# Adding the causal mask of the diagonal score tiles on VectorE, in PSUM, instead of by matmuls

## The chip, the cores and the metric

One core of one Trainium2 chip runs the whole program in one launch. The metric is the device time of an execution in microseconds (us). Three executions of the kernel before took 1168.46, 1168.53 and 1172.29 us; the median is 1168.53 us.

## The reference, cut to what matters

A block of four sequences of 1024 tokens (width 256): layer norm with modulation, attention, a residual, a second layer norm, a mixture of eight experts, a second residual. The change lies in the attention. There are 16 heads of 16 features. Of each head's query, key and value one feature per token is kept, the largest in magnitude; each query then keeps its 64 best allowed keys:

```python
q = _sparsify_last_dim_topk(proj(wq), feature_keep)     # feature_keep = 1
k = _sparsify_last_dim_topk(proj(wk), feature_keep)
v = _sparsify_last_dim_topk(proj(wv), feature_keep)
scores = einsum('bhqd,bhkd->bhqk', q, k) / sqrt(16)
causal = triu(ones((T, T), dtype=bool), k=1)
scores = where(causal[None, None], -inf, scores)         # a key later than the query is left out
topk_vals, topk_idx = lax.top_k(scores, 64)
attn = softmax(scatter of topk_vals, -inf elsewhere)
out = einsum('bhqk,bhkd->bhqd', attn, v)
```

## The kernel before, in words

**Tiles and groups.** The attention of one sequence b (0 to 3) and four heads g (0 to 3) is one of 16 groups, gi = 4 b + g. Keys lie on the 128 partitions, queries along the free dimension. A group has nine score units (table `UNITS`, line 330); a unit is 512 query columns, made of one or two pieces (i, t0, w): key tile i, queries from t0, width w. A piece whose first query is its tile's first key (t0 = 128 i) starts with a diagonal tile, 128 x 128, in which the keys later than the query must not count. There are eight such pieces in a group: two in units 0, 2 and 8, one in units 1 and 3. Units 4 to 7 have none.

**TensorE.** `scores(gi, u)` (line 436) writes the unit's four heads into two double banks of PSUM: half a = 0 holds heads 0 and 1, half a = 1 heads 2 and 3. For a piece it issues the products of query and key for four heads (line 451), then a product with `over` that pushes unselected keys down (455), and for a diagonal piece four matmuls of 128 columns (460) that add the tile `late`: 0 where the query may see the key, -1e30 where it may not. The last matmul of a half raises `f_full`. `late` is bf16 in SBUF and is filled once, before the attention starts.

**The ring.** Six banks are three double banks used in turn (`ring_at`, `begin`, line 369). A score unit takes two of them, other pieces of work (`chosen`, `project`, transposes) one each. The next unit therefore can't begin before ScalarE has read half a = 0 of the last one. Bank 6 gathers the output, bank 7 serves small work one piece at a time in a chain (`f_mfull`, `f_mfree`).

**ScalarE** waits for `f_full` and takes the exponential of half a unit at once (128 x 1024, line 850) into `p_buf`; its completion raises `f_free`. TensorE then multiplies `p_buf` with the values (`pv`, line 482).

**VectorE** works its own queue in program order (the loop from line 1166 on). For group gi this is: `mask` on unit 1 (two instructions of line 1068, after unit 1's exponentials and a matmul group `chosen`), `one_feature` for the next sequence (992, 997), `norm_stats`, or `second_norm` (1121, 1125) of the sequence before, `out_rows_of` (1073 to 1076), `key_counts` of the next group (1015, 1017), another `one_feature`, `mask` on unit 4, `keys` (1024 to 1032), `queries` (1037 to 1039), `zero_rank` (1044, 1047), `losers` (1054) and `negatives` (1060). Which of them exist depends on g: `one_feature` in g = 1 and 2 of b = 0 to 2 (four times a group); `second_norm` in g = 3 of b > 0; `norm_stats` in g = 0 (b < 3) and g = 1; `residual` (1101 to 1112) in g = 0 of b > 0, its second half just before `negatives`. TensorE waits for `mask` on unit 4 before `scores(gi, 5)`, since it frees the double banks, and for `losers` before the matmuls `lost` (432, 433) that end a group.

Every order is written out by hand; no planner or scheduler moves anything. These lines say the order around the change on VectorE, for a group's first third:

```python
                    mask(gi, 0, 0)
                    mask(gi, 0, 1)
                    if tiles:
                        one_feature(b + 1, t0)
                    if g == 0 and pre:
                        norm_stats(b + 1, 0)
                    if g == 3 and post:
                        second_norm(b - 1, 0)
                    if gi:
                        out_rows_of(gi - 1, 1)
                    if more:
                        key_counts(n)
```

Of the kernel before, what the change touches and what calls it, by code (L numbers as in the profile page):

```python
# [5 lines left out]
ALU = mybir.AluOpType  # L6
# [7 lines left out]
P = 128  # L14
# [6 lines left out]
HG = 4  # L21
# [11 lines left out]
def build_kernel(nc, x, wq, wk, wv, wo, router_w, router_b, w1, b1, w2, b2, c, wmod, out):  # L33
    with ExitStack() as ctx:
# [3 lines left out]
        def sem(name):  # L38
            return ctx.enter_context(nc.semaphore(name))
# [280 lines left out]
        TINY = 1e-30  # L320
        FAR = 2.0 ** 60

        f_const, f_ones = sem("f_const"), sem("f_ones")
        f_x, f_xr, f_xfree = (sem(n) for n in ("f_x", "f_xr", "f_xfree"))
        f_var, f_rstd, f_xhat, f_hT, f_yev, f_one, f_keep, f_cnt = (sem(n) for n in (
            "f_var", "f_rstd", "f_xhat", "f_hT", "f_yev", "f_one", "f_keep", "f_cnt"))
# [13 lines left out]
        NU = len(UNITS)  # L340
# [2 lines left out]


        ring_at, m_at, pv_at = {}, {}, {}

        def buf(u):
            q = ring_at[u] % 3
# [2 lines left out]
        def full_of(u):  # L351
            return f_full[ring_at[u] % 3], ring_at[u] // 3 + 1
# [10 lines left out]
        with nc.Block() as blk:  # L363
            @blk.tensor
            def _(pe):
# [70 lines left out]
                def scores(gi, u):  # L436
                    par = gi % 2
                    if u == 0:
                        pe.wait_ge(f_kp, gi + 1)
                        pe.wait_ge(f_uq, gi + 1)  # L440
                    for a in range(2):
                        begin(("S", gi, u, a))
                    lo = 0
                    for i, t0, w in UNITS[u]:
                        diag = t0 == P * i
                        last = (i, t0, w) == UNITS[u][-1]
                        for h in range(HG):
                            r = slice(32 * h, 32 * h + 32)
                            o = buf(("S", gi, u, h // 2))[:, h % 2, lo:lo + w]
                            key = ks[r, par, :] if i == 0 else kd[r, par, P * i:P * i + P]  # L450
                            pe.matmul(o, key, qx[r, par, t0:t0 + w], start=True, stop=False)  # L451
                        for h in range(HG):
                            r = slice(32 * h, 32 * h + 32)
                            o = buf(("S", gi, u, h // 2))[:, h % 2, lo:lo + w]
                            m = pe.matmul(o, over[r, :], qm[r, par, t0:t0 + w], start=False, stop=not diag)  # L455
                            if h % 2 and last and not diag:
                                m.then_inc(full_of(("S", gi, u, h // 2))[0], 1)
                        for h in range(HG * diag):
                            o = buf(("S", gi, u, h // 2))[:, h % 2, lo:lo + P]
                            m = pe.matmul(o, identb[:, :], late[:, :], start=False, stop=True)  # L460
                            if h % 2 and last:
                                m.then_inc(full_of(("S", gi, u, h // 2))[0], 1)
                        lo += w
# [342 lines left out]
            def _(act):  # L806
# [36 lines left out]
                def exps(gi, u):  # L843
                    j = NU * gi + u - PB
                    if j >= 0:
                        act.wait_ge(f_pv, pv_at[j // NU, j % NU])
                    for a in range(2):
                        w = ("S", gi, u, a)
                        act.wait_ge(*full_of(w))
                        act.activation(p_of(gi, u)[:, 2 * a:2 * a + 2, :], buf(w), ACT.Exp, scale=0.25).then_inc(free_of(w)[0], 1)  # L850

                def out_bank(gi, c):
# [86 lines left out]
            def _(dve):  # L939
# [118 lines left out]
                def negatives(n):  # L1058
                    m_full(("W", n))
                    dve.tensor_tensor(neg_in[:, :, :], ps[:, 7, :].rearrange("p (h t) -> p h t", h=HG),  # L1060
                                      thr_w[:, :].unsqueeze(1).to_broadcast([P, HG, P]), ALU.is_ge).then_inc(f_mfree, 1)

                def mask(gi, c, a):
                    u = ("Z", gi, c, a)
                    dve.wait_ge(*free_of(("S", gi, FIRST[c], a)))
                    dve.wait_ge(*full_of(u))
                    pb = p_of(gi, FIRST[c])[:, 2 * a:2 * a + 2, :]
                    dve.scalar_tensor_tensor(pb, buf(u), 1.0, pb, ALU.is_gt, ALU.mult).then_inc(free_of(u)[0], 1)  # L1068
# [95 lines left out]
                for gi in range(GA):  # L1164
                    b, g = divmod(gi, NG)
                    n = gi + 1
                    more, pre, post = n < GA, b + 1 < B, b > 0
                    tiles = pre and g in (1, 2)
                    t0 = 4 * (g - 1)

                    if g == 0 and post:
                        gate_weights(b - 1)
                        take_weights(b - 1)
                    mask(gi, 0, 0)
                    mask(gi, 0, 1)
                    if tiles:
                        one_feature(b + 1, t0)
                    if g == 0 and pre:
# [8 lines that stand above are left out]
                        normalize(b + 1, 0)  # L1187
                    if tiles:
                        one_feature(b + 1, t0 + 1)
                    mask(gi, 1, 0)  # L1190
                    mask(gi, 1, 1)
                    if g == 3 and post:
                        second_norm(b - 1, 1)
                    if g == 1 and pre:
                        norm_stats(b + 1, 1)
                    if more:
                        keys(n)
                    if tiles:
                        one_feature(b + 1, t0 + 2)
                    out_rows_of(gi, 0)  # L1200
                    if g == 0 and post:
                        take_mod(b - 1)
                    if more:
                        queries(n)
                    if g == 0 and post:
                        residual(b - 1, 0)
                    if more:
                        zero_rank(n)
                    if g == 1 and pre:
                        normalize(b + 1, 1)  # L1210
                    if g == 0 and pre:
                        modulate(b + 1, 0)
                    if tiles:
                        one_feature(b + 1, t0 + 3)
                    if g == 3 and pre:
                        feature_limits(b + 1)
                    if more:
                        losers(n)
                    if g == 0 and post:
                        residual(b - 1, 1)  # L1220
                    if g == 1 and pre:
                        modulate(b + 1, 1)
                    if g == 3 and post:
                        router_max(b - 1)
                    if more:
                        negatives(n)
                    if g == 3 and post:
                        router_share(b - 1)
# [762 lines left out]
```

## Time and profile before

| | |
|---|---|
| median of three executions | 1168.53 us |
| profiled execution, its time | 1168.28 us |
| its span, first to last instruction | 1166.5 us |
| mean granted TensorE clock | 0.905 of full |
| busy: TensorE, VectorE, ScalarE, GpSimd | 84%, 56%, 43%, 16% |
| attention groups | from about 116 to 787 us of the span |

A busy share is an average over stages. The first 116 us prepare weights and the first sequence, the last 380 us are the experts; the change touches only what lies between. A row of a view of groups gives line, engine, operation, tiles, shapes, count, busy us and mean ns of one, then the idle time before and what ended it. A row of the timeline gives the start, the duration over all instructions merged in it, engine, line, tiles, and in brackets the idle time before it and what ended that.

### The profile page before, as it was taken

Reading aid. Unit: us, or ns where it says so; the run is one execution under the profiler, and the core shown is the slowest. Engines: PE = TensorE matmul, PEld = TensorE weight load, DVE = VectorE, ACT = ScalarE, POOL = GpSimd, SP = SyncE. Lnnn points to the kernel's source line nnn. Section 1 sums busy time; section 2 is a strip of 40 time slices with the busy share of each in tenths; the row PEclk is TensorE's granted clock in tenths of the full one; section 3 lists DMA queues with packets and bytes.
Section 4 is the critical chain, followed back from the end, with each engine's and each line's share of the span. In section 5 each row is a group of like instructions: output and inputs, shape, how many; then the busy total and the mean of one; then the engine's idle time right before and its main releaser. Section 6 shows DMA issues by size and latency. Waiting matters only on the chain. (4 is left out here: it accounts for less than half of the span.)

```text
span 1166.5 us, 19195 instructions
## 1 busy us (share of the span) xinstructions
PE 978.1 (84%) x7592; PEld 545.0 (47%) x7592; DVE 652.7 (56%) x1378; ACT 506.7 (43%) x680; POOL 186.3 (16%) x280
## 2 busy tenths in 40 slices
PE   6453899999999999899998999998501799999996
PEld 4222344444444445454445453446401476666664
DVE  2445657756657764759666556643367555554441
ACT  0043666777466774556675646660000111111120
POOL 1231003200012200013110000000000434334322
PEclk9675999999899998999999899997555799999998
DMA  2200000000010001010000210002271244342211
GB/s 91 73 18 1 1 19 20 1 2 1 1 55 19 1 1 41 34 55 2 1 2 1 74 37 1 2 1 75 72 278 68 57 105 109 106 109 40 24 15 22
DMA packets 35456, 47.75 MB, mean 41 GB/s; under 512 B 2010, under 2 KB 31778, under 8 KB 35234
## 3 DMA queue, kind: packets, MB, share of 16 engines
q1 hardware_dynamic: 29218, 37.93, 9.7%
q0 software_dynamic: 6144, 8.52, 4.4%
q8 instruction: 64, 1.05, 0.4%
q14 instruction: 30, 0.25, 0.1%
HBM read 33.73 MB, written 12.72 MB: 40 GB/s over the span
## 5 line engine op out<-in xcount | busy, mean ns | idle before, releaser
L850 ACT ACTIVATE p_buf<-ps 128x1024 f32<-128x1024 f32 x288 | 279.2, 1023 | 188.3 <-PE ps L460 124.0
L451 PE MATMUL ps<-qx,kd 32*128 32x512 f32 (+3 forms) x1280 | 146.3, 527 | 23.6 <-DVE p_buf L1068 19.8
L482 PE MATMUL ps<-p_buf,vv 128*17 128x512 f32 (+3 forms) x1664 | 157.0, 479 | 0.0
L1824 ACT ACTIVATE h_t<-ps,b_t 128x512 f32<-128x512 f32 x64 | 44.0, 687 | 244.3 <-PE ps L1764 244.3
L1068 DVE SCALAR_TENSOR_TENSOR p_buf<-ps,p_buf 128x1024 f32<-128x1024 f32 x64 | 76.1, 1221 | 81.6 <-ACT p_buf L850 75.5
L1764 PE MATMUL ps<-tok_t,w_sb 128*128 128x512 f32 x256 | 114.1, 604 | 0.0
L1774 PE MATMUL ps<-w_sb,h_t 128*128 128x256 f32 x512 | 112.5, 380 | 0.8 <-ACT h_t L1824 0.8
L1774 PEld LDWEIGHTS ps<-w_sb,h_t 128*128 128x128 f32 x512 | 96.6, 190 | 15.3 <-ACT h_t L1824 1.6
L397 PE MATMUL ps<-w_t,h_t 128*128 128x512 f32 (+1 forms) x256 | 93.7, 514 | 8.8 <-DVEq L986 8.6
L451 PEld LDWEIGHTS ps<-qx,kd 32*128 32x128 f32 x1280 | 52.5, 189 | 64.5 <-issue 47.4
L1764 PEld LDWEIGHTS ps<-tok_t,w_sb 128*128 128x128 f32 x256 | 49.2, 194 | 59.2 <-issue 58.9
L784 POOL TENSOR_TENSOR qk<-y_val,y_one 128x512 f32<-128x512 f32 x32 | 37.1, 1159 | 238.2 <-DVE y_one L997 238.2
L397 PEld LDWEIGHTS ps<-w_t,h_t 128*128 128x128 f32 x256 | 48.4, 197 | 56.4 <-issue 51.4
L455 PE MATMUL ps<-qm,over 32*128 32x512 bf16 (+3 forms) x768 | 68.2, 328 | 0.0
L817 ACT ACTIVATE y_abs<-ps 128x768 f32<-128x768 f32 x32 | 25.9, 810 | 93.8 <-PE ps L397 87.4
L1728 POOL DMA_INDIRECT out_dram<-ctr,ids x32 | 50.7, 1583 | 98.1 <-issue 98.1
L482 PEld LDWEIGHTS ps<-p_buf,vv 128*17 128x17 f32 x1664 | 34.5, 97 | 55.6 <-issue 48.3
L460 PEld LDWEIGHTS ps<-late,identb 128*128 128x128 bf16 x512 | 29.9, 100 | 53.2 <-issue 53.2
L776 POOL TENSOR_TENSOR rstd<-var_e,half_neg 128x8 f32<-128x8 f32 x4 | 6.5, 1636 | 296.9 <-DVE var_e L1112 296.9
L1876 DVE TENSOR_TENSOR eo<-ps,b_sb 128x256 f32<-128x256 f32 x32 | 13.6, 425 | 72.0 <-PE ps L1774 71.4
L992 DVE TENSOR_REDUCE y_mx<-y_abs 128x48 f32<-128x768 f32 x32 | 30.5, 952 | 41.5 <-ACT y_abs L817 41.5
L460 PE MATMUL ps<-late,identb 128*128 128x128 bf16 x512 | 52.5, 227 | 0.0
(249 smaller groups left out, 1444.9 us busy)
## 6 DMA issues: line engine op xcount, KB each, us to landing
w_sb<-in_L_ffn_w_dram SPq DMA_DIRECT2D x16, 1024.0 KB, 8.6
h_table<-xr SPq DMA_DIRECT2D x4, 1056.0 KB, 4.6
x_in<-in_L_attn_x_dram SPq DMA_DIRECT2D x8, 512.0 KB, 3.5
xr<-in_L_attn_x_dram SPq DMA_DIRECT2D x4, 1024.0 KB, 5.5
out_dram<-xr SPq DMA_DIRECT2D x4, 1024.0 KB, 4.8
wmod_sb<-in_L_wmod_dram SPq DMA_DIRECT2D x1, 1536.0 KB
b_sb<-in_L_ffn_b_dram SPq DMA_DIRECT2D x1, 1024.0 KB, 9.5
gb_sb<-gb_table SPq DMA_DIRECT2D x1, 512.0 KB, 10.2
```

Source lines behind the costliest of these rows:

```text
L397: m = pe.matmul(buf(u)[:, bank, 0:n], h_t[:, k, (t % 4) * P:(t % 4 + 1) * P], w_t[:, k, lo:lo + n], start=k == 0, stop=k == KD - 1)
L451: pe.matmul(o, key, qx[r, par, t0:t0 + w], start=True, stop=False)
L455: m = pe.matmul(o, over[r, :], qm[r, par, t0:t0 + w], start=False, stop=not diag)
L460: m = pe.matmul(o, identb[:, :], late[:, :], start=False, stop=True)
L482: m = pe.matmul(ps[32 * h:32 * h + HD + 1, 6, o:o + w], vv[:, (gi // NG) % 2, i, HG * (gi % NG) + h, :], p_of(gi, u)[:, h, lo:lo + w], sta ...
L784: pool.tensor_tensor(qk[:, t], y_val[:, 0:2 * NH], y_one[:, 0:2 * NH], ALU.mult)
L850: act.activation(p_of(gi, u)[:, 2 * a:2 * a + 2, :], buf(w), ACT.Exp, scale=0.25).then_inc(free_of(w)[0], 1)
L1068: dve.scalar_tensor_tensor(pb, buf(u), 1.0, pb, ALU.is_gt, ALU.mult).then_inc(free_of(u)[0], 1)
L1728: pool.indirect_dma_start(out_rows, bass.IndirectOffsetOnAxis(ids[:, e, k:k + 1], 0), ctr[:, e % 2, k, :], None, compute_op=ALU.add).then_ ...
L1764: m = pe.matmul(ps[:, L1_BANKS[f % 3], :], w1_sb[:, e % WB, k, f * P:(f + 1) * P], tok_t[:, e % 2, k, :], start=k == 0, stop=k == KD - 1)
L1774: m = pe.matmul(ps[:, 4 + q % 2, 0:D], h1_t[:, f, q * P:(q + 1) * P], w2_sb[:, e % WB, f, :], start=f == 0, stop=f == FO - 1)
L1824: act.activation(h1_t[:, f, :], ps[:, L1_BANKS[f % 3], :], ACT.Relu, bias=b1_t[:, e * FO + f:e * FO + f + 1]).then_inc(s_h1, 1)
```

## The change

The matmuls with `late` (line 460) go. `scores` now raises `f_full` with its `over` product. VectorE adds `late` to the two heads of a half in place in PSUM, one instruction of 128 x 2 x 128 for each diagonal piece and half, and raises a new semaphore `f_late`; for units 0, 1, 2, 3 and 8 ScalarE waits for that instead of `f_full`. So 512 matmuls of TensorE leave and 256 instructions of VectorE come, 32 and 16 a group. Their places in VectorE's queue are those of the five calls of `set_late`. What is computed stays the same.

```diff
+        DIAG = tuple(u for u in range(NU) if any(t0 == P * i for i, t0, w in UNITS[u]))
+        late_at = {(gi, u, a): 2 * (len(DIAG) * gi + DIAG.index(u)) + a + 1 for gi in range(GA) for u in DIAG for a in range(2)}
...
-                            m = pe.matmul(o, over[r, :], qm[r, par, t0:t0 + w], start=False, stop=not diag)
-                            if h % 2 and last and not diag:
-                                m.then_inc(full_of(("S", gi, u, h // 2))[0], 1)
-                        for h in range(HG * diag):
-                            o = buf(("S", gi, u, h // 2))[:, h % 2, lo:lo + P]
-                            m = pe.matmul(o, identb[:, :], late[:, :], start=False, stop=True)
+                            m = pe.matmul(o, over[r, :], qm[r, par, t0:t0 + w], start=False, stop=True)
                             if h % 2 and last:
                                 m.then_inc(full_of(("S", gi, u, h // 2))[0], 1)
...
-                        act.wait_ge(*full_of(w))
+                        if u in DIAG:
+                            act.wait_ge(f_late, late_at[gi, u, a])
+                        else:
+                            act.wait_ge(*full_of(w))
...
+                def set_late(gi, u):
+                    for a in range(2):
+                        w = ("S", gi, u, a)
+                        dve.wait_ge(*full_of(w))
+                        lo = 0
+                        for i, t0, n in UNITS[u]:
+                            if t0 == P * i:
+                                s = buf(w)[:, :, lo:lo + P]
+                                m = dve.tensor_tensor(s, s, late[:, :].unsqueeze(1).to_broadcast([P, 2, P]), ALU.add)
+                            lo += n
+                        m.then_inc(f_late, 1)
...
+                    set_late(gi, 0)
+
                     if g == 0 and post:
                         gate_weights(b - 1)
                         take_weights(b - 1)
+                    set_late(gi, 1)
                     mask(gi, 0, 0)
                     mask(gi, 0, 1)
+                    set_late(gi, 2)
+                    set_late(gi, 3)
                     if tiles:
                         one_feature(b + 1, t0)
...
                     if tiles:
                         one_feature(b + 1, t0 + 3)
+                    set_late(gi, 8)
...
                     if more:
                         losers(n)
```

How this moves VectorE's queue is seen best in its rows. First the early part of a group with g = 2, before: `mask` on unit 1, `one_feature`, `out_rows_of`, `key_counts`, `one_feature`, `mask` on unit 4.

```order
L1068 SCALAR_TENSOR_TENSOR p_buf<-ps,p_buf 128x1024 x2
L992 TENSOR_REDUCE y_mx<-y_abs 128x48
L997 TENSOR_TENSOR y_one<-y_abs,y_mx 128x768
L1073 TENSOR_TENSOR z_lo<-z_lo,ps 128x16
L1074 RECIPROCAL o_inv<-ps 128x16
L1076 TENSOR_TENSOR o_tok<-ps,o_inv 128x4x64
L1015 TENSOR_SCALAR k_not<-kd 128x1024
L1017 SCALAR_TENSOR_TENSOR left<-k_not,minus 128x1024
L992 TENSOR_REDUCE y_mx<-y_abs 128x48
L997 TENSOR_TENSOR y_one<-y_abs,y_mx 128x768
L1068 SCALAR_TENSOR_TENSOR p_buf<-ps,p_buf 128x1024 x2
```

The same stretch now (lines below the new function are 12 higher, so `mask` is line 1080):

```order
L1071 TENSOR_TENSOR ps<-ps,late 128x2x128 x6
L1080 SCALAR_TENSOR_TENSOR p_buf<-ps,p_buf 128x1024 x2
L1071 TENSOR_TENSOR ps<-ps,late 128x2x128 x6
L992 TENSOR_REDUCE y_mx<-y_abs 128x48
L997 TENSOR_TENSOR y_one<-y_abs,y_mx 128x768
L1085 TENSOR_TENSOR z_lo<-z_lo,ps 128x16
```

Six additions stand ahead of the first `mask` (units 0 and 1) and six behind it (four for unit 2, two for unit 3), so everything from `one_feature` on comes after unit 3's scores. Next the end of a group with g = 0 and b > 0 on VectorE and the start of the group behind it, before: `zero_rank`, `modulate`, `losers`, second half of `residual`, `negatives`, `mask`.

```order
L1047 RECIPROCAL wk_r<-z_rank 128x128
L983 TENSOR_SCALAR h_t<-ps,mod_t 128x512 x2
L1054 SCALAR_TENSOR_TENSOR lw<-ps,y_mx,tie 128x128 x4
L1101 TENSOR_TENSOR xr<-ps,xr 128x4x256
L1106 BN_STATS st<-xr 128x6 x4
L1109 BN_AGGR mv<-st 128x2 x4
L1112 TENSOR_SCALAR var_e<-mv 128x8
L1060 TENSOR_TENSOR neg_in<-ps,thr_w 128x512
L1068 SCALAR_TENSOR_TENSOR p_buf<-ps,p_buf 128x1024 x2
```

And now:

```order
L1047 RECIPROCAL wk_r<-z_rank 128x128
L983 TENSOR_SCALAR h_t<-ps,mod_t 128x512 x2
L1071 TENSOR_TENSOR ps<-ps,late 128x2x128 x4
L1054 SCALAR_TENSOR_TENSOR lw<-ps,y_mx,tie 128x128 x4
L1113 TENSOR_TENSOR xr<-ps,xr 128x4x256
L1118 BN_STATS st<-xr 128x6 x4
L1121 BN_AGGR mv<-st 128x2 x4
L1124 TENSOR_SCALAR var_e<-mv 128x8
L1060 TENSOR_TENSOR neg_in<-ps,thr_w 128x512
L1071 TENSOR_TENSOR ps<-ps,late 128x2x128 x6
```

Unit 8's four additions stand ahead of `losers` in every group, and the next group's unit 0 is served only behind `residual` and `negatives`.

## Rows read from the trace of the kernel before

**Rows 1.** The page, part 1: busy us of each engine.
```profile
PE 978.1 (84%) x7592; PEld 545.0 (47%) x7592; DVE 652.7 (56%) x1378; ACT 506.7 (43%) x680; POOL 186.3 (16%) x280
```
**Rows 2.** Groups g = 2, 3, 0: length, busy PE, PEld, DVE, ACT, POOL, granted clock, DMA.
```profile
368.00:411.60 43.60, 41.89 (x371) 19.25 (x367) 29.25 (x38) 30.15 (x41) 8.39 (x9) 1.00 0.04 13
411.60:458.10 46.50, 41.78 (x401) 23.51 (x399) 27.41 (x52) 27.27 (x37) 0.00 (x0) 0.95 0.00 1
458.10:507.80 49.70, 46.65 (x399) 23.93 (x397) 30.26 (x62) 25.17 (x31) 1.01 (x1) 0.91 0.14 44
```
**Rows 3.** Groups of instructions by line.
```profile
L460 PE MATMUL ps<-late,identb 128*128 128x128 bf16 x512 | 52.5, 227 | 0.0
L1076 DVE TENSOR_TENSOR o_tok<-ps,o_inv 128x256 f32<-128x256 f32 x32 | 13.6, 425 | 2.4
```
**Rows 4.** Timeline of TensorE, unit 2 of the group g = 2, b = 1.
```profile
379.49 0.40 PE L460 MATMUL ps<-late,identb 128*128 128x128 bf16 x4
379.81 0.71 PE L451 MATMUL ps<-qx,kd 32*128 32x256 f32 x8
```
**Rows 5.** Timeline, units 0 and 1 of the last group.
```profile
754.79 0.93 PE L451 MATMUL ps<-qx,kd 32*128 32x384 f32 x8
...
757.02 1.94 ACT L850 ACTIVATE p_buf<-ps 128x1024 f32<-128x1024 f32 x2 [3.02 <-PE ps L460]
758.18 1.14 PE L451 MATMUL ps<-qx,ks 32*128 32x512 f32 x8 [0.17 <-ACT p_buf L850]
```
**Rows 6.** Timeline, group g = 2, b = 1, unit 3 to unit 5.
```profile
379.68 0.95 DVE L992 TENSOR_REDUCE y_mx<-y_abs 128x48 f32<-128x768 f32 x1 [2.17 <-ACT y_abs L817]
382.33 1.14 PE L451 MATMUL ps<-qx,kd 32*128 32x512 f32 x8
384.50 0.17 DVE L1073 TENSOR_TENSOR z_lo<-z_lo,ps 128x16 f32<-128x16 f32 x1 [2.76 <-PE ps L524]
391.07 2.35 DVE L1068 SCALAR_TENSOR_TENSOR p_buf<-ps,p_buf 128x1024 f32<-128x1024 f32 x2
392.44 1.14 PE L451 MATMUL ps<-qx,kd 32*128 32x512 f32 x8 [0.72 <-DVE p_buf L1068]
```
**Rows 7.** Timeline, end of the same group.
```profile
406.68 0.93 PE L451 MATMUL ps<-qx,kd 32*128 32x384 f32 x8
407.63 0.95 DVE L992 TENSOR_REDUCE y_mx<-y_abs 128x48 f32<-128x768 f32 x1 [0.60 <-ACT y_abs L817]
409.91 1.13 DVE L1054 SCALAR_TENSOR_TENSOR lw<-ps,y_mx,tie 128x128 bf16<-128x128 f32 x4 [0.22 <-PE ps L424]
411.09 0.23 PE L432 MATMUL ps<-upto,lw 128*128 128x128 bf16 x1 [0.24 <-DVE lw L1054]
```
**Rows 8.** Timeline, group g = 3, b = 1.
```profile
421.09 1.67 DVE L1121 SCALAR_TENSOR_TENSOR xr<-xr,mv,bc 128x256 f32<-128x256 f32 x4
425.96 0.17 DVE L1073 TENSOR_TENSOR z_lo<-z_lo,ps 128x16 f32<-128x16 f32 x1 [1.45 <-PE ps L524]
431.32 1.14 PE L451 MATMUL ps<-qx,kd 32*128 32x512 f32 x8 [0.99 <-DVE p_buf L1068]
447.00 1.13 DVE L1054 SCALAR_TENSOR_TENSOR lw<-ps,y_mx,tie 128x128 bf16<-128x128 f32 x4 [0.52 <-PE ps L424]
```
**Rows 9.** Timeline, group g = 0, b = 2, and the start of the next.
```profile
474.58 0.17 DVE L1073 TENSOR_TENSOR z_lo<-z_lo,ps 128x16 f32<-128x16 f32 x1 [2.34 <-PE ps L524]
482.54 1.14 PE L451 MATMUL ps<-qx,kd 32*128 32x512 f32 x8 [2.54 <-DVE p_buf L1068]
...
510.04 1.94 ACT L850 ACTIVATE p_buf<-ps 128x1024 f32<-128x1024 f32 x2 [6.26 <-PE ps L460]
510.86 0.68 DVE L1060 TENSOR_TENSOR neg_in<-ps,thr_w 128x512 bf16<-128x512 f32 x1
```
**Rows 10.** Stretches of 5 us around TensorE's wait of rows 9.
```profile
478.00:483.00 5.00, 2.46 (x18) 1.70 (x22) 4.88 (x8) 2.94 (x4) 0.00 (x0) 1.00 0.00 0
483.00:488.00 5.00, 5.00 (x37) 1.91 (x30) 4.27 (x6) 2.51 (x3) 0.00 (x0) 0.66 0.00 0
```

More of the change, by code:

```diff
@@ L321, in build_kernel @@
         FAR = 2.0 ** 60
-        f_const, f_ones = sem("f_const"), sem("f_ones")
+        f_const, f_ones, f_late = sem("f_const"), sem("f_ones"), sem("f_late")
         f_x, f_xr, f_xfree = (sem(n) for n in ("f_x", "f_xr", "f_xfree"))
@@ L444, in scores @@
                     for i, t0, w in UNITS[u]:
-                        diag = t0 == P * i
                         last = (i, t0, w) == UNITS[u][-1]
```

## The prediction

> **What bounds the kernel now.** I read the page first: TensorE is busy 84% of the span, VectorE 56% [rows 1]. The stretches then say what the average hides: in a group of the attention TensorE is busy 41.9 of 43.6 us, VectorE 29.3 [rows 2]. The reader is to see TensorE nearly full, and VectorE with a third of its time free. That makes the trade look sound: take work from the full engine, give it to the one with room. So the timeline has to say where TensorE does wait, since a shorter TensorE only moves such waits. It shows three. After unit 0 it waits 0.17 us for the exponential that frees a double bank [rows 5]. Before unit 5 it waits for VectorE's `mask`: 0.72 us in a group with g = 2, 0.99 in one with g = 3, 2.54 in one with g = 0 [rows 6, 8, 9]. Before `lost` it waits 0.24 us for `losers` [rows 7]. The last two are ends of long runs of VectorE in program order. VectorE's free time lies elsewhere, just ahead of instructions that wait for somebody: 2.17 us before `one_feature`, 2.76 before `out_rows_of` [rows 6]. The question is thus not whether 7 us of additions a group fit, but what they push behind them.
>
> **What is removed.** Four `late` matmuls begin 0.32 us before the next work begins [rows 4]; the 227 ns of one [rows 3] is its latency, and they overlap. 128 such sets are 128 x 0.32 = 41 us of TensorE, 2.6 a group. That is the most that could be won, and only where TensorE, not a wait, sets the pace.
>
> **What is added.** The trace has no addition in place in PSUM. The nearest row reads the same 256 elements from PSUM beside an SBUF operand: 425 ns [rows 3]. Its destination is SBUF, not PSUM. The bound below is 0.28 us, what `losers` takes per instruction in a run (four of half the size in 1.13 us [rows 7]); above, 0.6, should a write to PSUM cost again what the fixed part of the read does (an estimate: 425 ns less 128 ns for each further 128 elements leaves some 0.17). I take 0.42 for one and 0.38 in a run of four or more, as `second_norm` paces four of that size in 1.67 us [rows 8]: two additions 0.8, four 1.55 us. A group gets 16, so about 6.3 us. The Trainium skill (VectorE: DVE Perf Modes, the section on the TRN2 errata) gives 120 cycles plus the elements at 0.96 GHz for a PSUM source, 0.39 us, and advises tiles of 512 elements and up since each instruction pays its fixed part. By that figure, called an estimate, the sum below would be about 3 us lower; the row decides.
>
> **Units 0 to 3: a wait for a wait.** Unit 0 starts at 754.79 and ScalarE at 757.02, 2.23 us later [rows 5]. Without the matmuls the scores are complete 0.65 us sooner, at 1.58; two additions 0.8 and a hop of 0.05 bring ScalarE to 2.43. So the exponential is 0.2 us later, and unit 1, which waits for it, too. Unit 1 has one piece: 0.33 less, 0.5 more, again 0.15 late. Units 2 and 3 come out within 0.2 of before. None of the eight sets removed shortens the path here: the additions sit in the same loop from bank to exponential to bank. With `project` behind unit 1 (g = 1, 2) the delay is absorbed, since TensorE has 2.8 us of other work.
>
> **The queue behind unit 3, g = 1 and 2 of three sequences.** This is the largest term. `one_feature` ran at 379.68, in a gap, well ahead of `out_rows_of` at 384.50 [rows 6]. Now it is queued behind the additions to unit 3. Unit 3 starts at 382.33, less 0.1; complete after 1.3, two additions 0.8: VectorE is free at 384.4. Then `one_feature` 2.0, `out_rows_of` 0.8, `key_counts` 3.1, `one_feature` 2.0: `mask` on unit 4 can begin at 392.3, not 391.07 [rows 6]. TensorE's unit 5 is 1.2 us later. TensorE is full from there to unit 8 (406.68 [rows 7]), so 1.2 is carried. At the end `one_feature` waits for its own input (407.63 + 1.2), ends at 410.9; now four additions, 1.55; then `losers`, 1.15. `lost` starts at 413.7, not 411.09 [rows 7]: 2.6 late. Own-key, value and `turn_x` matmuls don't cover it. Six groups x 2.6 = 15.6.
>
> **g = 3 of b = 1 and 2.** `second_norm` (two runs of 1.7) ran from 421.09 in the gap before `out_rows_of` at 425.96 [rows 8]. Unit 3's additions end at about 426.1, so it now runs 426.1 to 429.5; `out_rows_of` is 3.5 late, and with no gap between, `mask` and unit 5 are too (431.32 to 434.8). VectorE then has no idle time until 0.52 before `losers` [rows 8], and four additions go in: 3.5 + 1.55 - 0.5 = 4.6. Two groups: 9.2.
>
> **g = 0 of b = 1 and 2.** `norm_stats` (2.1 us) was in the 2.34 before 474.58 [rows 9] and now begins at 474.4: unit 5 is 2.0 late. At the end `negatives` stands behind `residual`, which waits for TensorE; it began at 510.86, while ScalarE had begun unit 0 of the next group at 510.04 [rows 9]. The addition to that unit is behind it. Less 0.65 for unit 8's matmuls, `negatives` ends at 510.9 and ScalarE starts at 511.8: 1.7 late. Together 3.7, two groups 7.4.
>
> **The other six groups.** b = 0, g = 0: the same `norm_stats`, 2.3, and the run of rows 7's kind, 0.4 more: 2.7. b = 0, g = 3, no `second_norm`: 1.2. The last sequence: g = 0 without `norm_stats` 2.0 (mostly the 1.7 above), g = 1 and 2 0.6 each (0.35 as in units 0 and 1, the rest before `losers`), g = 3 2.0, since `second_norm` is pushed but `key_counts` is gone. Sum 9.1.
>
> **The clock.** TensorE waits 2.54 us in rows 9; in the 5 us behind, its granted clock is 0.66, so it falls from 2.4 to 1.2 GHz for about two thirds of the stretch [rows 10]. Longer waits (4.5 us before unit 5 in g = 3 and g = 0, 2 and 2.6 us twice in g = 1 and 2) may bring the same in other groups. A fall of 3.4 us (0.34 / 0.5 of 5) costs up to 1.7 where TensorE is full. I take three to four more that count: 5.5 us; ends 0 and 25.
>
> **Sum.** 15.6 + 9.2 + 7.4 + 9.1 + 5.5 = 46.8 us on the profiled execution's 1168.3: **1215 us**. The median of the runs shown is 0.25 us from that one, so it needs no correction. Additions at 0.28 (0.14 less on each of about eight exposed ones a group, 16 groups) give 18 less; at 0.6, 23 more.
>
> **Rivals.** *A, the pushed work isn't critical* (15%): only the loops of units 0 to 3, the additions before `losers` and behind `negatives` count, some 1 to 1.5 us a group: 1168 + 20 = 1188. For it: much of VectorE's delay could be caught in gaps that I treat as filled. Against it: TensorE already waits for `mask` in every group [rows 6, 8, 9]. *B, the clock* (15%): waits of 2 us and more in every group halve TensorE's clock a few us each, and the attention runs partly at 1.2 GHz: 14 falls of 1.7 us instead of three, about 1215 + 20 = 1235. In a sentence beside it: the Trainium skill (TensorE: Matmul & The Clock Gate, Part 1) has idleness throttle the array and activity release it; rows 10 agree after 2.5 us, but waits of 1 us in rows 8 left 0.95 over the group [rows 2]. *C, faster* (5%): the additions run in VectorE's gaps and TensorE keeps its saving. It decides where an addition starts within 0.2 us of the scores' end and costs under 0.3: the exponential then comes 0.1 us sooner in every loop, and TensorE wins up to half of 41 us: 1168 - 20 = 1148. Against it: unit 8's additions are ahead of `losers`, on the path in nearly every group. *D, no change* (4%): the two balance, 1168; for it only that TensorE is full between the waits.
>
> **Chances and range.** My forecast, 1195 to 1235 about 1215, has 61%. The range that holds 8 in 10 takes in most of A and B: 1190 to 1242. A difference of 0.5%, 5.8 us, is about what a measurement can tell from none. Faster 0.05, within 0.5% 0.04, slower 0.91.
>
> **What would show it.** Right, step by step: TensorE's busy time down by about 50 us while its waits grow by more; `mask` before unit 5 ending TensorE's waits with 2 to 5 us in most groups; `losers` ending 2 to 3 us of wait before `lost` or `logits`; ScalarE waiting for the additions; 256 additions of 0.38 to 0.45 us; groups of g = 3 some 4 to 5 us longer, of g = 1 and 2 some 2.5, of the last sequence under 2. The prediction is wrong if `one_feature` and `second_norm` start later but unit 5 does not, if the additions take 0.3 us or less, if the attention's granted clock falls below 0.9 of full on average (rival B), or if the middle groups are no longer than before.

## The result, and the profile after

The changed kernel is slower, as forecast, by more than the sum said and inside the range: 1230.4 us (median of 4 runs, 1225.7 to 1234.6) against 1168.5 (median of 4, 1168.1 to 1172.3), a ratio of 1.052 with a 95% interval of 1.047 to 1.057. The forecast was 1215 (1190 to 1242).

| | before | after |
|---|---|---|
| median | 1168.5 us | 1230.4 us |
| profiled execution / its span | 1168.3 / 1166.5 us | 1227.7 / 1226.0 us |
| TensorE busy | 978.1 us | 964.5 us |
| VectorE busy | 652.7 us | 745.4 us |
| mean granted clock | 0.905 | 0.874 |

I account for the profiled execution, 59.4 us longer. First the page of the kernel after: busy time, and the costliest group that the change adds. [rows 1] is the line of before.

```profile
PE 964.5 (79%) x7080; PEld 534.7 (44%) x7080; DVE 745.4 (61%) x1634; ACT 507.5 (41%) x680; POOL 191.1 (16%) x280
...
L1071 DVE TENSOR_TENSOR ps<-ps,late 128x256 f32<-128x256 f32 x256 | 92.7, 425 | 100.1 <-PE ps L457 99.2
```

TensorE lost its 512 `late` matmuls, and yet its busy time fell by 13.6 us only: more of what is left of it ran at the half clock, and so took longer. VectorE has 92.7 us more. TensorE's idle share grew from 16% to 21%; VectorE's shrank from 44% to 39%.

The next view lists waits: who, for whom, total us, times, longest. Of before, those of TensorE and its exponential:

```profile
ACT p_buf L850 <- PE ps L460: 124.0, 69, 13.3
...
PE ps L451 <- DVE p_buf L1068: 19.8, 21, 2.5
...
PE ps L451 <- ACT p_buf L850: 6.6, 18, 1.1
PE ps L432 <- DVE lw L1054: 2.9, 8, 1.2
```

And of after (L453 is before's L451, L1080 its L1068, L435 its L432):

```profile
ACT p_buf L850 <- DVE ps L1071: 130.5, 68, 12.9
...
PE ps L453 <- DVE p_buf L1080: 41.5, 24, 4.4
PE ps L453 <- ACT p_buf L850: 35.3, 33, 3.3
...
PE ps L435 <- DVE lw L1054: 15.8, 11, 2.0
```

ScalarE now waits for the additions where it waited for the matmuls. TensorE waits 21.7 us more for `mask`, 28.7 more for the exponential and 12.9 more for `losers`. The rest of the account is the clock. Stretches of the attention, 660 us of each kernel (length, busy PE, PEld, DVE, ACT, POOL, granted clock, DMA, GB/s), before and then after:

```profile
140.00:800.00 660.00, 620.35 (x5723) 303.58 (x5719) 413.89 (x704) 413.30 (x542) 64.48 (x56) 0.97 0.06 18
```
```profile
140.00:800.00 660.00, 557.29 (x4780) 269.21 (x4784) 472.38 (x877) 386.11 (x510) 68.09 (x56) 0.92 0.05 16
```

0.05 of 660 us is 33 us of full clock not granted. The two stretches don't quite hold the same work: that of before ends 13 us behind the attention, that of after 46 us short of its end. So I sum the granted clock from the trace over the attention itself, up to its last `logits` (786 and 846 us) and without the low stretch in which its first group begins (it ends at 118 us before, at 130 after). There TensorE was at 1.2 GHz for 34 us in five falls before, and for 106 in 18 after. Twelve of the 18 come with TensorE's wait before unit 5, three with the wait before unit 1 in groups with g = 1, two lie in `logits`, one at a group's start.

**One middle group, step by step.** The group g = 2, b = 1, on the timeline of after; its lines answer to [rows 6, 7]:

```profile
390.04 0.93 PE L453 MATMUL ps<-qx,kd 32*128 32x384 f32 x8
...
391.17 0.69 DVE L1060 TENSOR_TENSOR neg_in<-ps,thr_w 128x512 bf16<-128x512 f32 x1 [0.30 <-issue]
...
391.78 1.42 DVE L1071 TENSOR_TENSOR ps<-ps,late 128x256 f32<-128x256 f32 x4
392.62 1.94 ACT L850 ACTIVATE p_buf<-ps 128x1024 f32<-128x1024 f32 x2 [2.03 <-DVE ps L1071]
...
393.79 1.14 PE L453 MATMUL ps<-qx,ks 32*128 32x512 f32 x8 [1.41 <-ACT p_buf L850]
...
405.38 0.76 DVE L1071 TENSOR_TENSOR ps<-ps,late 128x256 f32<-128x256 f32 x2 [1.98 <-PE ps L457]
406.05 0.94 DVE L992 TENSOR_REDUCE y_mx<-y_abs 128x48 f32<-128x768 f32 x1
...
409.95 2.60 DVE L1017 TENSOR_TENSOR_SCAN left<-k_not,minus 128x1024 bf16<-128x1024 bf16 x1
414.64 2.35 DVE L1080 SCALAR_TENSOR_TENSOR p_buf<-ps,p_buf 128x1024 f32<-128x1024 f32 x2
416.00 1.70 PE L453 MATMUL ps<-qx,kd 32*128 32x512 f32 x8 [1.98 <-DVE p_buf L1080]
...
431.84 0.93 PE L453 MATMUL ps<-qx,kd 32*128 32x384 f32 x8
...
434.76 1.42 DVE L1071 TENSOR_TENSOR ps<-ps,late 128x256 f32<-128x256 f32 x4
436.09 1.12 DVE L1054 SCALAR_TENSOR_TENSOR lw<-ps,y_mx,tie 128x128 bf16<-128x128 f32 x4
437.26 0.23 PE L435 MATMUL ps<-upto,lw 128*128 128x128 bf16 x1 [1.98 <-DVE lw L1054]
```

`one_feature` (L992), which ran in a gap before, stands right behind unit 3's additions; `mask` for unit 4 (L1080), and with it unit 5, end up late; and `losers` (L1054) stands behind unit 8's. With the starts of the units counted from that of unit 0 (368.10 before, 390.04 after) the group reads:

| start of, from unit 0's | before | after | later by |
|---|---|---|---|
| unit 1 | 3.40 | 3.75 | 0.35 |
| unit 3 | 14.23 | 13.96 | -0.27 |
| unit 5 | 24.34 | 25.96 | 1.62 |
| unit 6 | 30.40 | 33.61 | 3.21 |
| unit 8 | 38.58 | 41.80 | 3.22 |
| `lost` | 42.99 | 47.22 | 4.23 |

Up to unit 3 nothing is lost. Unit 5 is 1.6 late; from unit 5 to unit 6 another 1.6 is lost, though TensorE waits for nothing there (busy 5.00 of the 5 us below); and 1.0 before `lost`. The second of these is the clock. Stretches of 5 us, before and behind TensorE's wait at 416.00:

```profile
411.00:416.00 5.00, 2.02 (x20) 0.77 (x17) 4.74 (x5) 3.97 (x6) 1.20 (x2) 1.00 0.00 0
416.00:421.00 5.00, 5.00 (x33) 1.77 (x34) 4.92 (x7) 2.81 (x4) 0.59 (x1) 0.66 0.00 0
```

And the same place of the kernel before, where the wait was 0.72 us [rows 6]:

```profile
387.40:392.40 5.00, 4.03 (x32) 1.55 (x30) 4.41 (x5) 4.14 (x6) 1.16 (x2) 1.00 0.00 0
392.40:397.40 5.00, 4.96 (x36) 2.14 (x37) 4.93 (x7) 3.60 (x6) 0.63 (x2) 1.00 0.00 0
```

Behind a stretch with 2.02 us of TensorE work in five, the clock fell to 1.2 GHz for two thirds of the next; behind one with 4.03 it stayed at 2.4.

**A group with g = 3** (b = 1) shows the pushed `second_norm` (L1133), the 3.82 us wait before unit 5, and a loss that I had not seen, at its end:

```profile
451.19 0.77 DVE L1071 TENSOR_TENSOR ps<-ps,late 128x256 f32<-128x256 f32 x2 [1.98 <-PE ps L457]
451.86 1.67 DVE L1133 SCALAR_TENSOR_TENSOR xr<-xr,mv,bc 128x256 f32<-128x256 f32 x4
...
460.55 2.09 PE L453 MATMUL ps<-qx,kd 32*128 32x512 f32 x8 [3.82 <-DVE p_buf L1080]
...
479.87 0.61 PE L573 MATMUL ps<-rw_sb,o_t 128*128 128x8 f32 x4 [1.74 <-DVE lw L1054]
...
481.77 1.02 PE L573 MATMUL ps<-rw_sb,o_t 128*128 128x8 f32 x4
...
491.43 0.29 PE L435 MATMUL ps<-upto,lw 128*128 128x128 bf16 x1 [0.74 <-DVEq L1146]
```

From unit 0, unit 5 is 3.1 later than before (22.74 against 19.68), unit 6 4.7 (28.74, 24.00), `logits` (L573) 5.5 (42.06, 36.54), the next unit 0 8.1 (54.58, 46.50). `logits` (the scores by which tokens are routed to experts) is eight small sets of matmuls; from the third on each takes 1.02 us instead of 0.61. In the kernel before the same fall came at the seventh (two rows of it):

```profile
452.46 0.61 PE L576 MATMUL ps<-rw_sb,o_t 128*128 128x8 f32 x4
...
453.42 1.02 PE L576 MATMUL ps<-rw_sb,o_t 128*128 128x8 f32 x4
```

From the start of `logits` to the `lost` behind it: 9.00 us before, 11.56 after.

**By kind of group**, from one start of `negatives` to the next (the last group of a sequence up to the first `negatives` of the next), in us longer than before, against the forecast without its clock term: six groups g = 1, 2 of b = 0 to 2, 3.7, 4.6, 7.1, 4.6, 7.9, 6.0, in all 33.9 (forecast 15.6, and by this measure 19.0, since 1.7 us of the forecast for each g = 0 of b = 1, 2 fall into the g = 1 behind it); g = 3 of b = 1, 2, 8.1 and 8.9 (forecast 4.6 each); g = 0 of b = 1, 2, 0.5 and 0.6 (3.7 each, 2.0 by this measure). The other six groups together 7 (9.1), the last of them counted up to its `logits`.

### The profile page after: what moved, and what is told of

Its sections match the earlier page's. It is cut to its first block and busy times, and to the rows that moved or that the text cites. A ratio compares the mean times of both kernels' runs of the same rounds, so it can differ in the third digit from the quotient of the medians.

```text
span 1226.0 us, 18427 instructions
## 1 busy us (share of the span) xinstructions
PE 964.5 (79%) x7080; PEld 534.7 (44%) x7080; DVE 745.4 (61%) x1634; ACT 507.5 (41%) x680; POOL 191.1 (16%) x280
## 5 line engine op out<-in xcount | busy, mean ns | idle before, releaser
L453 PE MATMUL ps<-qx,kd 32*128 32x512 f32 (+3 forms) x1280 | 148.4, 539 | 54.0 <-DVE p_buf L1080 41.5
L479 PE MATMUL ps<-p_buf,vv 128*17 128x512 f32 (+3 forms) x1664 | 163.7, 497 | 0.0
L1071 DVE TENSOR_TENSOR ps<-ps,late 128x256 f32<-128x256 f32 x256 | 92.7, 425 | 100.1 <-PE ps L457 99.2
L453 PEld LDWEIGHTS ps<-qx,kd 32*128 32x128 f32 x1280 | 57.6, 197 | 99.2 <-issue 86.7
L1080 DVE SCALAR_TENSOR_TENSOR p_buf<-ps,p_buf 128x1024 f32<-128x1024 f32 x64 | 76.1, 1219 | 23.1 <-ACT p_buf L850 18.4
L457 PE MATMUL ps<-qm,over 32*128 32x512 bf16 (+3 forms) x768 | 72.6, 344 | 0.0
L814 ACT ACTIVATE y_abs<-ps 128x768 f32<-128x768 f32 x32 | 25.9, 810 | 101.0 <-PE ps L400 85.7
L1894 DVE TENSOR_TENSOR eo<-ps,b_sb 128x256 f32<-128x256 f32 x32 | 13.6, 425 | 72.2 <-PE ps L1792 71.6
L453 PE MATMUL ps<-qx,ks 32*128 32x512 f32 x256 | 38.1, 664 | 23.3 <-ACT p_buf L850 22.9
L992 DVE TENSOR_REDUCE y_mx<-y_abs 128x48 f32<-128x768 f32 x32 | 30.4, 950 | 33.0 <-ACT y_abs L814 32.3
## 6 DMA issues: line engine op xcount, KB each, us to landing
gb_sb<-gb_table SPq DMA_DIRECT2D x1, 512.0 KB, 10.2
```

What stands on the lines that cost most here:

```text
L479: m = pe.matmul(ps[32 * h:32 * h + HD + 1, 6, o:o + w], vv[:, (gi // NG) % 2, i, HG * (gi % NG) + h, :], p_of(gi, u)[:, h, lo:lo + w], sta ...
L1071: m = dve.tensor_tensor(s, s, late[:, :].unsqueeze(1).to_broadcast([P, 2, P]), ALU.add)
```

## Experiments

Each run is given as a ratio to the kernel before on the same chip. By it the changed kernel is at 1.052; 1% is 11.7 us. Three series were run, with kernels before at 1175.2, 1172.8 and 1168.6 us.

**What the matmuls are worth.** Mask left out for four of the five diagonal units:

```
- DIAG = tuple(u for u in range(NU) if any(t0 == P * i for i, t0, w in UNITS[u]))
+ DIAG = (0, 2, 3, 8)          # neither late matmuls nor set_late for these
```

> The late mask is left out for units 0, 2, 3 and 8 (neither matmul nor addition), so late keys of those tiles count in the output; unit 1 keeps its matmuls. It removes 112 of 128 sets, 112 x 0.32 = 36 us of TensorE, and adds nothing. If TensorE set the pace everywhere, 1168 - 36 = 1132 us. If its waits for VectorE (mask before unit 5, losers before lost) take part of it back, as I hold, 1140 to 1152 us.

1141.2 us, ratio 0.971 (0.967 to 0.975), 34 us less. A group has eight sets of four matmuls, one of them unit 1's, so 112 sets are left out: 112 x 0.32 = 36 us. I had expected part of it to be taken back; at the ratio, 1134 us in place of 1168.5, it is under my 1140 to 1152. The saving was not hidden: it was there almost in full for whoever would not spend it again.

**Both at once.** The additions, and the matmuls kept:

```
-  m = pe.matmul(o, over[r, :], qm[r, par, t0:t0 + w], start=False, stop=True)
+  m = pe.matmul(o, over[r, :], qm[r, par, t0:t0 + w], start=False, stop=not diag)
...
+  for h in range(HG * diag):
+      o = buf(("S", gi, u, h // 2))[:, h % 2, lo:lo + P]
+      m = pe.matmul(o, identb[:, :], late[:, :], start=False, stop=True)
```

> The changed kernel with the matmuls kept as well: both mask the same tiles, the output is the same. It prices the matmuls once the additions are there. No mask at all on units 0, 2, 3 and 8 was worth 34 us, so if the matmuls' price is the same beside the additions, 1.052 + 0.030 = 1.08 times the kernel before. If they lie beside VectorE's delay where TensorE waits for mask and losers, about a third to a half of them shows: 1.062 to 1.07.

This kernel adds `late` twice. 1266.1 us, ratio 1.079 (1.076 to 1.083). Against 1.052 the matmuls are still worth 2.7%, 32 us (the two intervals leave some 7 us either way), beside the additions. So the change won some 32 us and paid some 94 with the additions in their places; my sum had 41 at most and 88.

**Which unit's additions cost it.** Three kernels, each with the additions for some units and the matmuls for the others (`DIAG = (0, 1)`, `(2, 3)`, `(8,)`, and the old matmuls for `u not in DIAG`).

> Additions for units 0 and 1 only, matmuls for units 2, 3 and 8. Theory Q (what is pushed behind the additions in VectorE's queue is the loss): about 0.35 us a group from the loop, and 1.7 us at the three changes from g = 0 to g = 1 behind negatives: 1168 + 10 = 1178 us. Rival L (the loss is the longer loop from bank to exponential to bank wherever an addition sits in it): 3 of 8 pieces, 1168 + 23 = 1191 us.

Units 0 and 1: 1186.1 us, ratio 1.010 (1.006 to 1.014).

> Additions for units 2 and 3 only. Theory Q: mask before unit 5 is late by 1.2 us in six groups, 3.5 in two, 2 in three: 20 us, and with some falls of the clock 1168 + 28 = 1196 us; TensorE's waits before unit 5 as long as in the changed kernel. Rival L: 3 of 8 pieces, 1191 us, and no longer waits before unit 5.

Units 2 and 3: 1216.5 us, ratio 1.035 (1.032 to 1.038).

> Additions for unit 8 only. Theory Q: they stand ahead of losers, 1.2 to 1.5 us a group where TensorE waits for it, 12 groups: 1168 + 17 = 1185 us. Rival L: 2 of 8 pieces, 1168 + 15 = 1183 us, but with TensorE's wait before lost unchanged at 0.24 us. The times are too near to part the two; the wait before lost does.

Unit 8: 1185.0 us, ratio 1.010 (1.006 to 1.013).

11, 41 and 10 us, each good to about 4: the sum, 62, is the whole loss, so nothing shows that the three parts share a cost or hide one another. Theory Q had 10, 28 and 17, rival L 23, 23 and 15. Q fits units 0 and 1; for units 2 and 3 it was 13 us short and L 18, and for unit 8 both were too high. The waits decide between them. Two thirds come from units 2 and 3, which have six of a group's sixteen additions, the same number as units 0 and 1. The waits of the three kernels say where each pays; first units 0 and 1, in the exponential (6.6 before), then units 2 and 3, in `mask` (19.8 before), then unit 8, in `losers` (2.9 before):

```profile
PE ps L454 <- ACT p_buf L856: 27.1, 18, 3.4
```
```profile
PE ps L454 <- DVE p_buf L1088: 39.1, 20, 4.5
```
```profile
PE ps L435 <- DVE lw L1060: 17.8, 11, 2.0
```

**One line moved.** Unit 3's two additions behind `one_feature`, `norm_stats` and `second_norm`, all else as changed:

```
                     set_late(gi, 2)
-                    set_late(gi, 3)
...
+                    set_late(gi, 3)
```

> The changed kernel with one move alone: unit 3's additions behind one_feature, norm_stats and second_norm. Units 2 and 3 cost 41 us and the full reordering gave back 38 of the changed kernel's 62. If what unit 3 pushes is the larger part, ratio 1.028 to 1.038. If the gain came from unit 8 and unit 0, 1.045 or more.

1190.6 us, ratio 1.020 (1.017 to 1.023): 3.2%, 37 us of the 62 (some 7 us either way), from one line, more than the 1.028 to 1.038 that I had expected. The same group on its timeline (unit 0 at 373.80):

```profile
387.07 0.94 DVE L992 TENSOR_REDUCE y_mx<-y_abs 128x48 f32<-128x768 f32 x1
...
389.15 0.76 DVE L1071 TENSOR_TENSOR ps<-ps,late 128x256 f32<-128x256 f32 x2
...
397.80 1.14 PE L453 MATMUL ps<-qx,kd 32*128 32x512 f32 x8 [0.72 <-DVE p_buf L1080]
```

Unit 5 is 24.00 us behind unit 0, not 25.96 (before 24.34), unit 6 30.07, not 33.61 (before 30.40): the late start and the slow stretch behind it go together. The wait for `mask` over the whole run is 21.9 us, 19.6 less than in the changed kernel, and the time at half clock 58 us, 48 less, worth up to 24 where TensorE is full; 19.6 and at most 24 cover the 37.

**All three moved.** Unit 8's additions behind `losers` as well, and unit 0's of g = 1 ahead of the second half of `residual`:

```
-                    set_late(gi, 0)
+                    if not (g == 1 and post):
+                        set_late(gi, 0)
...
-                    set_late(gi, 8)
...
+                    set_late(gi, 8)
...
+                        set_late(gi + 1, 0)
```

> The same additions, all of them, in other places of VectorE's queue: unit 3's behind one_feature, norm_stats or second_norm instead of ahead of them; unit 8's behind losers; unit 0's of g = 1 ahead of the second half of residual. Theory Q: units 2 and 3 cost 41 us mostly by what they push, unit 8 and the change to g = 1 10 us each; two thirds of the loss of 62 comes back: ratio 1.015 to 1.025. Rival L (work and loop, whatever the place): ratio 1.045 or more.

1195.8 us, ratio 1.020 (1.018 to 1.022): the two further moves give nothing. With unit 3 moved alone, the `lost` matmuls waited 16.8 us in all for `losers`; now they wait 5.6. In its place the next unit 0 waits for its double bank, one instruction further: on TensorE's timeline the score units other than 1 and 4 wait 26.4 us for exponentials, not 11.5. Unit 1 waits less, and all waits of the attention together come to 88 us, against 91 with unit 3 moved alone, so little was left to win. The timeline of the group's end: unit 8's additions, its exponential, and the next unit 0, which needs the bank.

```profile
417.68 1.41 DVE L1071 TENSOR_TENSOR ps<-ps,late 128x256 f32<-128x256 f32 x4
418.53 1.94 ACT L850 ACTIVATE p_buf<-ps 128x1024 f32<-128x1024 f32 x2 [3.19 <-DVE ps L1071]
419.70 0.93 PE L453 MATMUL ps<-qx,kd 32*128 32x384 f32 x8 [1.25 <-ACT p_buf L850]
```

**The clock alone.** TensorE filled while it waits for `mask`: 8 matmuls of 512 columns, 16 in the groups with the longest waits (g = 0 of b = 0 to 2, g = 3 of b = 1, 2), into the bank that unit 5 will overwrite.

```
+ if u == 5 and a == 0:
+     for k in range(16 if (g == 3 and 0 < b < 3) or (g == 0 and b < 3) else 8):
+         pe.matmul(buf(("S", gi, u, 0))[:, k % 2, :], identb[:, :],
+                   onesz[:, :, :].rearrange("p h t -> p (h t)"), start=True, stop=True)
```

> The changed kernel, with 8 or 16 matmuls of 512 columns on constants written to unit 5's first double bank while TensorE waits for the second one (they are overwritten). Clock theory (the waits before unit 5 let the granted clock fall, and that costs 10 us or more): granted clock up from 0.874 to 0.885 or more and the time 8 to 20 us below the changed kernel, ratio to before 1.035 to 1.045. If the falls don't matter: ratio 1.05 or a little above.

1221.4 us, ratio 1.041 (1.038 to 1.045): 1.1% less than the changed kernel, 12.5 us (the two intervals leave some 7 us either way), with work added and no dependency changed. The stretch of the same group, at full clock throughout where the changed kernel had 0.96:

```profile
388.10:435.00 46.90, 41.65 (x356) 18.87 (x359) 35.52 (x55) 30.77 (x43) 8.57 (x8) 1.00 0.04 12
```

Unit 5 starts 25.88 us behind unit 0 (25.96 in the changed kernel), the next group's unit 0 46.11 (47.77): unit 5 is as late as it was, and the 1.7 us behind it are gone.

Over the attention, time at half clock is 58 us, not 106, so the 12.5 us are for 48 of the 72 us that the change added. In proportion the whole clock term is 19 us (an estimate), where I took 5.5. The 12.5 are net of what the filler itself costs where it outlasts the wait: in g = 0, b = 1, unit 5 is 28.01 us behind unit 0 and was 23.99. The filler doesn't mend `logits`: the falls there are longer still, 17.1 us each (10.2 before, 13.7 in the changed kernel), and 17.1 too with unit 3 moved. So the fall in `logits` doesn't hang on the waits before unit 5; why it comes sooner stays open.

**Another engine.** If the mask on the exponential's far side is as good, GpSimd, busy 16%, can do it: it multiplies the diagonal 128 columns of the exponentials in SBUF by the 0/1 matrix `upto`. Unit 1 keeps its matmuls.

```
+ def not_late(gi, u):
+     for a in range(2):
+         pool.wait_ge(*free_of(("S", gi, u, a)))
...
+             s = p_of(gi, u)[:, :, lo:lo + P]
+             m = pool.tensor_tensor(s, s, upto[:, :].unsqueeze(1).to_broadcast([P, HG, P]), ALU.mult)
...
+     m.then_inc(f_pm, 1)
```

First for units 0, 2, 3 and 8:

> From the kernel before: matmuls with late leave units 0, 2, 3 and 8 and GpSimd multiplies the exponentials in SBUF by 0 or 1 instead, one instruction of 128 x 512 for each diagonal piece, between ScalarE and the products with the values; nothing is added between bank, exponential and bank. 7 instructions of about 1.2 us a group on GpSimd. If the place outside the loop is what counts, most of the 34 us of the run without a mask: ratio 0.97 to 0.985. If GpSimd is late for the values (units 2 and 3 have about 2 us between exponential and use) or slows VectorE: 0.99 to 1.02.

1164.6 us, ratio 0.992 (0.989 to 0.995). The matmuls' 34 us are won and most of them lost again. Groups of instructions, GpSimd's new one and VectorE's scan:

```profile
L803 POOL TENSOR_TENSOR p_buf<-p_buf,upto 128x512 f32<-128x512 f32 x112 | 146.2, 1326 | 332.2 <-ACT p_buf L876 328.8 <-issue 3.3
```
```profile
L1043 DVE TENSOR_TENSOR_SCAN left<-k_not,minus 128x1024 bf16<-128x1024 bf16 x16 | 48.8, 3048 | 1.5 <-issue 0.4
```

The scan takes 3.05 us instead of 2.29, beside GpSimd's work on units 2 and 3; `mask` stands behind it and TensorE waits 35.4 us for it in all, 15.6 more than before. So units 2 and 3 were given back to the matmuls:

> GpSimd masks the exponentials of units 0 and 8 only, matmuls for 1, 2 and 3. 64 of 128 sets are gone, up to 19 us at the 34 per 112 measured. With GpSimd beside it VectorE's scan of line 1043 takes 3.05 us instead of 2.29, and it is on the way to mask before unit 5; the work for units 0 and 8 lies in VectorE's gap before mask on unit 1 instead. So ratio 0.983 to 0.989, the scan back at 2.3 us. If the slowing of VectorE was not what limited the first GpSimd kernel: 0.992 or above.

1147.7 us, ratio 0.983 (0.980 to 0.986), the shortest with the one that follows. The scan is as it was, and GpSimd's product is quicker too:

```profile
L804 POOL TENSOR_TENSOR p_buf<-p_buf,upto 128x512 f32<-128x512 f32 x64 | 72.7, 1157 | 353.4 <-ACT p_buf L875 352.0 <-issue 1.4
...
L1042 DVE TENSOR_TENSOR_SCAN left<-k_not,minus 128x1024 bf16<-128x1024 bf16 x16 | 36.7, 2291 | 1.5 <-issue 0.4
```

Two more kernels put unit 3's product behind the scan, GpSimd waiting until `mask` is half through unit 4 (`pool.wait_ge(*free_of(("Z", gi, 1, 0)))`): with units 0, 3 and 8, and with units 0, 2, 3 and 8.

> As before it, and unit 3 too, its work held until mask on unit 4 has begun to finish (so behind key_counts). 80 sets gone, up to 24 us: ratio 0.979 to 0.986. If GpSimd is then late for the values of unit 3, no better than with units 0 and 8 alone.

1147.3 us, ratio 0.983 (0.980 to 0.985): the third unit adds nothing that can be measured.

> Units 0, 2, 3 and 8 on GpSimd as in the first such kernel, but unit 3 held back as well. Unit 2's two instructions still lie beside out_rows_of and second_norm. 112 sets gone: ratio 0.978 to 0.988 if only the scan matters; 0.99 or above if unit 2's place does.

1154.3 us, ratio 0.985 (0.980 to 0.990). The first of the four, with the same units, was at 0.992: 0.7% for holding unit 3's product back, with intervals that just overlap, so it isn't shown. The scan takes 2.57 us on average there, since unit 2's product still falls beside it, and TensorE waits 25.9 us for `mask`, not 35.4. Whether the remaining distance to 0.971 can be had was not tried further.

## Why the prediction was right, and where its sum was short

**The sign, and the reason for it, held.** TensorE's saving is spent again by work pushed down VectorE's queue: rival C (faster) and D (no change) fall with the separate kernels, A (the pushed work isn't critical) with the single line that moves it and is worth 37 us.

**The removal: held.** 41 us at most, 36 for the four units tried, 34 measured.

**The addition: held.** 0.425 us alone and 1.42 for four, forecast 0.42 and 1.55. The row that reads PSUM and writes SBUF [rows 3] told it exactly; the estimate from the Trainium skill (VectorE: DVE Perf Modes, the section on the TRN2 errata) of 0.39 was 8% low.

**Units 0 to 3: half held.** In g = 2 the exponential is 0.35 later, counted from unit 0, not 0.2: I had overlooked that `negatives` is ahead of the addition in VectorE's queue (391.17, then 391.78). It is made up by unit 3, as "absorbed" said. Over the run units 0 and 1 alone cost 11 us net, where I had counted them for little outside the change from g = 0 to g = 1. At that change the forecast was 1.7 us; from unit 0 to its exponential it is now 4.49 us and was 2.23 (as in [rows 5]), 2.3 later (g = 1, b = 2):

```profile
546.32 1.41 DVE L1071 TENSOR_TENSOR ps<-ps,late 128x256 f32<-128x256 f32 x4
547.16 1.94 ACT L850 ACTIVATE p_buf<-ps 128x1024 f32<-128x1024 f32 x2 [6.51 <-DVE ps L1071]
```

**The queue behind unit 3, middle groups: held, 0.4 short.** "TensorE's unit 5 is 1.2 us later": it is 1.6. What I can name for the rest: GpSimd's `keep` (its products for `one_feature`) now falls beside `key_counts`, whose scan L1017 takes 2.60 us there, not 2.29, and whose L1015 takes 1.12, not 0.69. Before `lost` 1.4 was forecast and 1.0 came. Together 2.6, as the forecast had it. What the group lost beyond that, 1.6, it lost between unit 5 and unit 6.

**g = 3: held to `logits`.** Unit 5 3.1 later (forecast 3.5), unit 5 and the additions before `logits` 3.1 + 0.8 = 3.9 without the slow stretch (forecast 4.6).

**g = 0: too much.** From unit 0, unit 5 is 0.75 later in b = 2 (25.15 against 24.40), not 2.0. The delay of VectorE is there, since the wait before unit 5 grew by 1.9, from 2.54 to 4.41 us. But TensorE comes to unit 4 1.1 us sooner (16.22, 17.33), probably by the matmuls that it no longer has: I had followed the delay and not the saving. In b = 1 unit 5 is 1.7 later (23.99 against 22.27), near the forecast, and 1.2 us of that is made up by the start of the next group.

**The clock: the step that failed.** "I take three to four more that count: 5.5 us." The falls went from 5 to 18. Each middle group has one behind unit 5: four pay 1.6 us between unit 5 and unit 6, the other two 2.4 and 2.9, in all 11.7. Each g = 3 of b = 1 and 2 pays 1.7 there (from 3.1 to 4.7 in the first) and 2.6 and 2.3 from `logits` to the next group, 8.3 for the two. That is 20, near the 19 of the filler's estimate. With 19 for 5.5 the sum would be 1229, against 1227.7 for the profiled execution. That it comes so near is partly luck: the middle groups lost some 3 us more than forecast even without the clock, and g = 0 and the other six groups some 5 less. This is rival B's mechanism, priced there at 20 more, in about the size that it gave (1235). The reason I gave against it, that waits of 1 us left 0.95 over a group, misread the row: what lowered that group's clock was the fall in its `logits` at 453 us, and no fall came with its wait before unit 5. It was also beside the point, since the change made those waits 2 us. The Trainium skill (TensorE: Matmul & The Clock Gate, the section on HAM oscillation) tells of a kernel that is throttled again at every tile, by a wait in each; the trace here agrees, with 18 falls in 16 groups.

**What it would show.** TensorE's busy time was to fall by about 50 us and fell by 13.6. The 52.5 us of the `late` matmuls [rows 3] overlap (41 us by their starts; the kernel with 112 of the 128 sets left out was busy 35.9 less), and matmuls at half clock take longer. The attention's clock stayed at 0.92, so the mark that I set for rival B, below 0.9, was too low: most of B's price came above it.

## What to carry to other kernels

Before work is moved to an engine with room, read that engine's instructions in order, and ask of each place where the new one goes what stands behind it and who waits for that: here the same additions, one line later, cost 37 us less. Where the wait of a nearly full TensorE grows from one to two us, price the slower stretch behind it beside the wait itself. And the engine that has the most room and no one behind it (GpSimd, for two of the five units) can turn the same idea into 1.7%, if what it runs beside is left alone.

## What the runs showed that I had not expected

- A wait of 1.98 us in a full kernel is followed by the clock at 1.2 GHz (0.66 over the next 5 us), one of 0.72 by none. Filler matmuls in the wait gained 12.5 us of 1230, good to about 7.
- `logits`, matmuls of 8 columns with TensorE nearly always busy by the profile (11.26 of 12 us), ran mostly at half clock, in the kernel before too; what moved was where the fall came:

```profile
480.00:492.00 12.00, 11.26 (x54) 10.80 (x55) 0.45 (x2) 0.26 (x1) 0.00 (x0) 0.55 0.00 0
```
```profile
448.00:458.00 10.00, 9.07 (x56) 8.60 (x56) 0.58 (x3) 0.26 (x1) 0.00 (x0) 0.76 0.00 0
```

- A scan of VectorE from bf16 to bf16 took 3.05 us beside GpSimd's products and 2.29 alone; the products 1.33 us on average there and 1.16 in the kernel where none ran beside it. The second scan, which reads f32, stayed at 2.28, but no product ran beside it in that kernel. In the kernel with units 0, 3 and 8, where one did in groups with g = 2, it took 3.25. So holding unit 3's product back moved part of the price from one scan to the other. The Trainium skill (GPSIMD Engine Reference, section 2) has GpSimd's ports to SBUF shared with VectorE; the trace agrees for both scans.
- The costs of the three parts added up almost exactly (11 + 41 + 10 against 62), though each of them changes the clock as well. With some 4 us of noise on each, part of that is luck.
